# FFN gate and up products of blocks 2 to 6: seven block products in place of eight

## The reference

```python
def block(x, W_qkv, b_qkv, W_out, b_out):               # x: (2, 1024, 512) float32
    x = x + causal_attention(layernorm(x), 16 heads of 32) @ W_out.T + b_out
    h = layernorm(x)
    return x + (silu(h @ w_gate.T) * (h @ w_up.T)) @ w_down.T   # w_gate, w_up: (2048, 512)
```

## Time and profile before

| | before |
|---|---|
| median of 3 runs | 2179.28 us (2178.76 to 2180.1) |
| profiled execution, its own time | 2179.44 us |
| its span | 2177.7 us |
| TensorE matmul busy | 2113.8 us, 97% |
| VectorE busy | 1253.6 us, 58% |
| ScalarE busy | 530.9 us, 24% |
| GpSimd busy | 668.9 us, 31% |
| mean granted TensorE clock | 0.997 |

### The profile page before, as it was taken

The page is one execution under the profiler, slowest core; times in us unless marked ns, Lnnn a source line. Parts: engine busy times, 40 slices in busy tenths (PEclk is TensorE's granted clock), DMA queues, the critical chain, the costliest instruction groups (busy, mean ns, idle before and its releaser), DMA issues.

```text
span 2177.7 us, 34223 instructions
## 1 busy us (share of the span) xinstructions
PE 2113.8 (97%) x11056; PEld 1486.4 (68%) x11056; DVE 1253.6 (58%) x2476; ACT 530.9 (24%) x1076; POOL 668.9 (31%) x508
## 2 busy tenths in 40 slices
PE   6999999999999999999989999999999999999998
PEld 5555478888755548888865554888877554588886
DVE  6766564544676647444467665644456767454445
ACT  1344420000144441000014454100011444310001
POOL 3324233332312323323231233333323223233322
PEclk9999999999999999999999999999999999999999
DMA  4333111111323211111242321111113232111113
GB/s 130 94 79 79 31 36 52 49 58 39 79 70 79 70 31 49 50 48 49 68 129 70 79 69 40 39 59 39 49 40 81 68 81 68 40 49 49 59 39 97
DMA packets 59748, 135.15 MB, mean 62 GB/s; under 512 B 10784, under 2 KB 11808, under 8 KB 59552
## 3 DMA queue, kind: packets, MB, share of 16 engines
q1 hardware_dynamic: 59552, 132.71, 21.6%
HBM read 77.62 MB, written 4.19 MB: 38 GB/s over the span
## 4 chain that ended last, share of the span: by engine, by line
PE 88%; issue 5%; DVE 2%; POOL 2%; ACT 1%; DMA 1%; SPq 0%; DVEq 0%; POOLq 0%; ACTq 0%
PE ring L898 13%; PE ring L899 13%; PE ring L900 13%; PE bank L1011 13%; PE ring L965 8%; PE bank L989 7%; PE bank L898 7%; PE bank L900 7%; PE bank L899 7%; PE ring L889 1%; ACT prob L560 1%; DMA area<-nm_lo 1%; POOL area L438 1%; DVE xn L699 1%; POOL prob L463 1%
## 5 line engine op out<-in xcount | busy, mean ns | idle before, releaser
L898 PE MATMUL ring<-xt_hi,area 128*128 128x512 f32 x1248 | 489.8, 392 | 1.1 <-DVE kq_parts L688 1.1
L899 PE MATMUL ring<-xt_lo,area 128*128 128x512 f32 x1248 | 486.4, 390 | 0.0
L900 PE MATMUL ring<-xt_hi,area 128*128 128x512 f32 x1248 | 486.0, 389 | 0.0
L699 DVE CUSTOM_DVE_ANT_0 xn<-ring,mask_row 128x128 bf16<-128x128 f32 (+7 forms) x512 | 374.5, 749 | 99.9 <-PE ring L965 93.9
L560 ACT ACTIVATE prob<-bank 128x512 f32<-128x512 f32 (+3 forms) x768 | 335.0, 489 | 342.4 <-PE bank L989 341.6
L436 POOL TENSOR_SCALAR area<-w_stage 128x1024 fp32r<-128x1024 f32 x131 | 144.4, 1103 | 762.2 <-PE bank L900 404.7
L766 DVE TENSOR_TENSOR prob<-prob,ring 128x512 f32<-128x512 f32 x128 | 87.8, 686 | 456.9 <-ACT prob L578 456.9
L438 POOL TENSOR_TENSOR area<-w_stage,area 128x1024 fp32r<-128x1024 f32 x131 | 322.8, 2464 | 10.9
L578 ACT ACTIVATE prob<-ring 128x512 f32<-128x512 f32 x128 | 76.5, 598 | 970.4 <-PE ring L900 970.4
L898 PEld LDWEIGHTS ring<-xt_hi,area 128*128 128x128 f32 x1248 | 234.3, 188 | 59.1 <-issue 9.8
L900 PEld LDWEIGHTS ring<-xt_hi,area 128*128 128x128 f32 x1248 | 234.3, 188 | 49.1
(11 more groups left out here) (78 smaller groups left out, 2053.4 us busy)
## 6 DMA issues: line engine op xcount, KB each, us to landing
w_stage<-ffn_w SPq DMA_DIRECT2D x96, 512.0 KB, 3.3
area<-kq_parts SPq DMA_DIRECT2D x336, 128.0 KB, 2.4
w_stage<-attn_w SPq DMA_DIRECT2D x35, 512.0 KB, 3.3
x<-x_in SPq DMA_DIRECT2D x24, 256.0 KB, 3.9
area<-attn SPq DMA_DIRECT2D x48, 128.0 KB, 2.3
out<-x SPq DMA_DIRECT2D x16, 256.0 KB, 2.2
bias_rows<-row_bias SPq DMA_DIRECT2D x10, 256.0 KB, 4.2
area<-nm_hi SPq DMA_DIRECT2D x32, 8.0 KB, 1.8
```

The costliest lines, as they stand in the source:

```text
L699: dve.tensor_tensor_reduce(out=sum_out[:, RING[name] % 2, 0:keys], in0=src[:, 0:keys], in1=mask_row[:, TOKENS - keys:], scale=1.0, scalar= ...
L898: pe.matmul(dst, ah, bh, start=first and k == 0, stop=False)
L899: pe.matmul(dst, ah, bl, start=False, stop=False)
L900: ins = pe.matmul(dst, al, bh, start=False, stop=last and k == n - 1)
```

## The change

Let W be the weight of a block (gate or up), cut into W11, W12, W21, W22 (tile by half of the 512 inputs), and X the transposed x, cut into halves by chunks. For blocks 2 to 6 ("quads") both steps of a block are formed together by Winograd's form of the 2x2 product with seven products of 6 matmuls each:

- GpSimd forms S1 = W21 + W22, S3 = W11 - W21, S2 = S1 - W11, S4 = W12 - S2 from the staged weight (four 256-column instructions) and splits the four sums as it splits a weight (`quad_sums`, `s_split`), ahead of the plain split of the same slot. The sums lie in a ring of four buffers.
- VectorE forms four differences of X in six 1024-column instructions (`diff_sum`), ScalarE their high parts, VectorE their low parts (`diff_to_lo`, 1024 columns, four of them). They are put between the steps 2 and 3 (`DIFFS_BESIDE`). For their sake `xt_to_hi` writes a second, full copy of the late half of x^T (`xt_late`), ahead of the high part.
- TensorE sums m1, m6, m5, m3 up in one PSUM pair ("x"), m7 and m4 in a second ("y"), m2 alone in a third ("z"). ScalarE copies the state of x behind m1, m6 and m5 to SBUF (`keep`); VectorE adds these copies to y, z and y (`quad_add`). ScalarE makes the high part of the hidden tiles (`quad_hi`).
- The down rows of a block follow in the next block, behind m7, m6, m5 and m2, in two PSUM banks in place of four. Those of block 6 stand between and behind the gate_up of step 14.
- At the end of an iteration GpSimd writes ones over 2 x 6144 elements again, since the sums have lain there.

```diff
+PRODUCTS = ("m1", "m7", "m6", "m5", "m2", "m3", "m4")
+OUTPUTS = ((1, 1), (0, 0), (0, 1), (1, 0))
+DIFFS_BESIDE = ((((("sum", 0), ("sum", 1)), (("sum", 2), ("sum", 3), ("lo", 0))),
+                ((("sum", 4), ("lo", 1)), (("sum", 5), ("lo", 2)))))
+ROWS_BEHIND = ("m7", "m6", "m5", "m2")
...
 def xt_to_hi(it, name):
+                if name in (("ln2", 2), ("ln2", 3)):
+                    late = xt_late[:, :, 2 * (r - 2) * P:2 * (r - 1) * P].rearrange("p k (t n) -> p k t n", n=P)
+                    act.activation(late, src, ACT.Copy)
                 act.activation(dst, src, ACT.Copy).then_inc(xt_hi_ready, 1)
...
 def split_weights(it, i):
+                if part < 2 and QUAD_FIRST <= b <= QUAD_LAST:
+                    quad_sums(it, b, part, w_stage[:, j % 2, :])
+                    s_split(it, b, part)
...
+                pool.tensor_tensor(s1, a21, a22, ALU.add).then_inc(s_step, 1)
+                pool.tensor_tensor(s3, a11, a21, ALU.subtract).then_inc(s_step, 1)
+                wait_alone(pool, s_step, s_steps(it, b, w, 0))
+                pool.tensor_tensor(s2, s1, a11, ALU.subtract).then_inc(s_step, 1)
+                wait_alone(pool, s_step, s_steps(it, b, w, 2))
+                pool.tensor_tensor(s4, a12, s2, ALU.subtract).then_inc(s_step, 1)
...
+                pool.tensor_scalar(both[:, 0, :, :], sums, 1.0, 0.0, ALU.mult, ALU.add
+                                   ).then_inc(s_step, 1)
+                pool.tensor_tensor(both[:, 1, :, :], sums, both[:, 0, :, :].bitcast(F32),
+                                   ALU.subtract)
...
                 for i in range(FFN_SLOT0 + 3, SLOTS + 2):
                     split_weights(it, i)
+                wait_alone(pool, product_full, products(it, QUAD_LAST, "m3", 1))
+                wait_alone(pool, w_split, it * SLOTS + SLOTS + 2)
+                pool.memset(k_stack[3 * HEAD:3 * HEAD + 2, 1:, :, :].bitcast(F32), 1.0).then_inc(ones_ready, 1)
...
 # VectorE
+                def quad_block(b):
+                    add_rows(2 * b - 1)
+                    quad_add(b, (1, 1), 0)
+                    quad_add(b, (1, 1), 1)
+                    if b > QUAD_FIRST:
+                        add_rows(2 * b - 2, range(2))
+                    quad_multiply(b, (1, 1))
+                    quad_add(b, (0, 0), 0)
+                    quad_add(b, (0, 0), 1)
+                    quad_lo(b, (1, 1))
+                    if b > QUAD_FIRST:
+                        add_rows(2 * b - 2, range(2, CT))
+                    quad_multiply(b, (0, 0))
+                    quad_lo(b, (0, 0))
+                    quad_multiply(b, (0, 1))
+                    quad_lo(b, (0, 1))
+                    quad_add(b, (1, 0), 0)
+                    quad_add(b, (1, 0), 1)
+                    quad_multiply(b, (1, 0))
+                    quad_lo(b, (1, 0))
...
+                for s in range(1, QUAD_STEPS[0]):
                     for t in range(BT):
                         hidden_parts(s, t)
+                        if s >= QUAD_STEPS[0] - 2:
+                            for what, n in DIFFS_BESIDE[s - QUAD_STEPS[0] + 2][t]:
+                                (diff_sum if what == "sum" else diff_to_lo)(n)
                     for d in downs_after(s):
+                        add_rows(d)
+                diff_to_lo(3)
+                for block_at in range(QUAD_FIRST, QUAD_LAST + 1):
+                    quad_block(block_at)
...
 # TensorE
+                    if m == "m1":
+                        pe.wait_ge(w_split, it * SLOTS + FFN_SLOT0 + 3 * b + w + 1)
+                        if b == QUAD_FIRST:
+                            pe.wait_ge(rows_drained, rows_taken(it, row_at(2 * b - 2, w)))
...
+                    rows = [late[0:2], late[2:4], [(2 * b - 2, 0), (2 * b - 2, 1)], [(2 * b - 2, 2), (2 * b - 2, 3)]]
+                    if b == QUAD_FIRST:
+                        rows = [[one] for one in late]
+                    for m in PRODUCTS:
+                        for w in range(2):
+                            product(b, m, w)
+                        if m in ROWS_BEHIND:
+                            for s, t in rows[ROWS_BEHIND.index(m)]:
+                                down_row(s, t)
...
+                for b in range(QUAD_FIRST, QUAD_LAST + 1):
+                    quad_block(b)
+                for t in range(BT):
+                    gate_up(STEPS - 2, t)
+                    down(STEPS - 4 + t)
+                down(STEPS - 2)
```

More of the change, by code:

```diff
@@ L85, in downs_after @@
 def downs_after(s):
-    return {0: (0,), 1: (), STEPS - 2: (s - 1, s), STEPS - 1: (s,)}.get(s, (s - 1,))
+    return {0: (0,), 1: ()}.get(s, (s - 1,))
 EARLY = {1: 2, 3: 12, 5: 12, 7: 12}
@@ L137, in ring_order @@
     yield from (("gu", 0, 0), ("gu", 0, 1), ("ln2", 2), ("ln2", 3))
-    yield from (("gu", s, t) for s in range(1, STEPS) for t in range(BT))
+    yield from (("gu", s, t) for s in range(1, STEPS) for t in range(BT) if s not in QUAD_STEPS)
 TAKE_AFTER = (8, 17)
@@ L424, in split_weights @@
                     after = last_product(before)
-                    if after[0] == "rows":
+                    if after[0] == "product":
+                        wait_alone(pool, product_full, products(it, *after[1:]))
+                    elif after[0] == "rows":
                         wait_alone(pool, rows_full, it * ROWS + after[1] + 1)
@@ L449, in last_product @@
                 x_last = b * CHUNKS + CHUNKS - 1
-                return ("rows", x_last * CT + CT - 1) if part == 2 else ("gu", x_last, BT - 1)
+                if part == 2:
+                    return "rows", max(row_at(b * CHUNKS + c, CT - 1) for c in range(CHUNKS))
+                return ("product", b, "m4", part) if QUAD_FIRST <= b <= QUAD_LAST else ("gu", x_last, BT - 1)
             def inverse_deviation(it, ln, c):
@@ L755, in add_projected, with add_rows @@
                     tile_stats(t)
-                def add_rows(row, t, b):
-                    dve.wait_ge(rows_full, it * ROWS + row + 1)
-                    dve.tensor_tensor(x[:, t, :], x[:, t, :], bank[b][:, :], ALU.add).then_inc(rows_drained, 1)
+                def add_rows(s, tiles=range(CT)):
+                    for n in tiles:
+                        dve.wait_ge(rows_full, it * ROWS + row_at(s, n) + 1)
+                        t = s % CHUNKS * CT + n
+                        dve.tensor_tensor(x[:, t, :], x[:, t, :], row_bank(s, n)[:, :], ALU.add
+                                          ).then_inc(rows_drained, 1)
@@ L892, in iteration, with three @@
             def iteration(it):
-                def three(dst, terms, first=True, last=True):
+                def three(dst, terms, first=True, last=True, more=False):
                     n = len(terms)
                     for k, (ah, al, bh, bl) in enumerate(terms):
-                        pe.matmul(dst, ah, bh, start=first and k == 0, stop=False)
-                        pe.matmul(dst, ah, bl, start=False, stop=False)
-                        ins = pe.matmul(dst, al, bh, start=False, stop=last and k == n - 1)
+                        pe.matmul(dst, ah, bh, start=first and k == 0, stop=False, skip_group_check=more)
+                        pe.matmul(dst, ah, bl, start=False, stop=False, skip_group_check=more)
+                        ins = pe.matmul(dst, al, bh, start=False, stop=last and k == n - 1, skip_group_check=more)
                     return ins
@@ L1046, in gate_up @@
                     pe.wait_ge(ring_drained, buffer_free(it, ("gu", s, t)))
+                    if s == STEPS - 2:
+                        quads_left(1 + t)
                     for w in range(2):
@@ L1053, in down @@
                 def down(s, tiles=range(BT)):
[L1054 to L1057, removed]
                     for t in range(CT):
[L1059 to L1070, removed]
+                        down_row(s, t, tiles)
@@ L1161, in iteration @@
                     down(0, range(t, t + 1))
-                for s in range(1, STEPS - 1):
+                for s in range(1, QUAD_STEPS[0]):
                     for t in range(BT):
```

255 lines of the change are left out of this document (241 added, 14 removed).

## The result

The changed kernel takes 2212.76 us (median of 4, 2212.38 to 2219.56) against 2179.02 before: a ratio of 1.0163, 95% interval 1.0147 to 1.0179. It is slower by 34 us, where 2182 was forecast with a range that ended at 2210. The profiled execution took 2212.88 us, its span is 2210.8.

What follows compares the result with a forecast made beforehand. TensorE, busy 97% of the span, was taken as the bound. -54.4 + 35.2 (entry) + 6.4 (clock) + 3.2 (FFN start) + 12.0 (exit) = +2.4 on 2179.44 gave 2181.8, stated as 2182 us; 8-in-10 range 2138 to 2210.

Steps and rivals of the forecast that it cites:

- What is removed: Gate and up of five blocks: 240 matmul slots fewer, 54.4 us saved; a quad lasts 29.92 us.
- GpSimd in a quad: Quads: 256-column two-input instruction 0.73 us, 28.2 of 29.92 us filled per block, no stall from GpSimd in quads 3 to 6.
- Rival 2: Quads: GpSimd becomes the bound, m1 waiting for weights; 2202 us at 1.0 us per sum, 2219 at 1.1; chance 0.19.
- Entry: Before the first m1: GpSimd's 22.6 and VectorE's 13.7 us add up from 324.3; wait 8.8 us per iteration, 35.2 in all.
- Exit: Behind quad 6: a down row waits for the last hidden tile's low part, 3.0 us late, 12.0 in all.
- Start of the FFN: ScalarE's extra 1024-column copy ahead of the high part delays TensorE by 0.8 us, 3.2 in all.
- VectorE and ScalarE in a quad: Inside the quads: VectorE about 15 us, ScalarE 8.4 us; smallest margin 1.6 us in the hidden tiles' chain, no stall.
- The clock term: Behind the entry wait: about eight matmuls at the lower clock, 1.6 us each time, 6.4 in all, bounds 0 and 12.8.

Runs made afterwards that it cites:

- e1: Changed kernel with GpSimd's weight sums and their split left out, TensorE taking plain weight parts instead; 2198.8 us (ratio 1.0099 to the kernel before).
- e7: Changed kernel with VectorE's additions of down(2)'s rows taken ahead of the last difference sum and its low part; 2206.5 us (ratio 1.0120).
- e4: Changed kernel with the six difference sums moved to step 1, their high parts with them, and low parts spread behind hidden tiles; 2177.7 us (ratio 0.9995).
- e3: Changed kernel with both gate_up tiles of step 14 placed before down(12) behind the last quad; 2195.8 us (ratio 1.0077).
- e2: Changed kernel with the first quad's down rows in pairs behind m7 and m6, not one behind each of four products; 2195.6 us (ratio 1.0081).
- e5: Changed kernel with 36 matmuls without use put into the wait in front of the first m1; 2205.0 us (ratio 1.0118).
- e8: Changed kernel with GpSimd's sums and their split replaced by constant writes that read nothing, TensorE taking plain weight parts; 2194.2 us (ratio 1.0068).
- e6: Changed kernel with the edits of e2, e3 and e4 together; 2135.3 us (ratio 0.9800).

## Why the prediction was wrong, point by point

- *What is removed*: right; 240 matmuls, 29.92 us per quad.
- *GpSimd in a quad*: right. A 256-column instruction takes 0.73 to 0.75 undisturbed (0.73 forecast), and a block keeps GpSimd busy for 24.5 us in quads that TensorE never waits in (28.2 forecast, gaps and waits included). Rival 2 is refuted as the cause, though the time lies where it would have put it: the list has no wait for a weight part.
- *Entry*: the wait is 8.6 us per iteration (8.8 forecast), 34.2 in all (35.2). The size was right, the reason only in part, and so the close hit is in part luck. The sum added up the work of two engines from 324.3 on. It left out that the last tile's chain can't start before its gate and up products are done. Without GpSimd's sums and their split it would have given no wait at all (324.3 + 9.6 + 13.7 + 0.6 = 348.2, ahead of 353.1), and e1 still measured 5.1. So the sums' backlog is 3.5 of the 8.6, and the rest is an order without slack that meets plain splits: e7 takes 3.3 away by order alone, e4 7.5 by order and place together. (The sum also has five casts where its own count of 18 instructions leaves four, 0.28 too much.)
- *Exit*: 3.2 us per iteration, 12.7 in all (12.0); e3 confirms the place.
- *Start of the FFN*: 2.0 in all (3.2).
- *VectorE and ScalarE in a quad: "The smallest margin is 1.6 us: no stall"*: this step failed. It was worked out for a quad whose rows come in pairs, and carried over to the first quad, whose four rows are spread to behind m2 while VectorE's order keeps them all in front of `quad_add`. I had the edit in the diff (`rows = [[one] for one in late]`) and followed only its weight place, not the queue behind it. Cost: four waits of 3.15 (12.6 us), 1.0 for m6 once, and 10.1 us of slowed matmuls behind them, some 24 of the 31 us that the forecast is off by. e2 shows it.
- *The clock term*: mis-sized. I took 6.4 us, for the entry alone, with 12.8 as its upper end; measured are 25.4 in the four stages. By place they are 8.6 at the entry, 10.1 at the second quad and 6.3 at the exit. At the entry the price was near (1.6 each forecast, 1.9 by e5, 2.0 to 2.4 by the trace), but it is paid after short waits too: behind the exit's 3.2 us in all four iterations, behind the second quad's 3.15 us in three of four. The sentence that the shorter exit wait may not pay, which I drew from the Trainium skill (TensorE: Matmul & The Clock Gate, "What's actually happening"), does not hold here: 3.2 us were enough.

The sum, mended with these: -54.4 + 62.5 + 25.4 = +33.5 where +2.4 stood. Of the missing 31, 14 are the second quad's waits and 19 the clock; entry and exit differ by 1, and against these stand the 3.2 of the FFN's start, which the +2.4 has and the 62.5 has not. What remains open is why a wait of one length sometimes leaves the clock alone. It isn't bound to the place: the second quad's wait left it alone in the first iteration of the changed kernel, but halved it there in e1, e3, e4, e5 and e7, and the exit's left it alone in two iterations of e4 and one of e1. That e2 saved 17 us where its FFN stages fell by 22 is the part outside the stages, which is 5.2 us longer in its trace. Whether the changed kernel's own low 1173.5 there is chance or an effect of the change, no run shows.

## What to carry to other kernels

Where a change takes matmuls off a TensorE that never pauses, look first at the seams, in front of the first and behind the last of the new pieces, and ask which of its waits have no slack there. In this kernel the steady state was covered from the first version on. Follow each queue there by itself, with its own order; a piece that differs from the others by one line has a chain of its own. Put VectorE's work with two SBUF inputs where GpSimd doesn't read SBUF, and price waits of TensorE like those met here (2.9 to 8.7 us) at their length plus 1.3 to 3.3 us for the clock, which nearly all of them cost.

## What the runs showed of the hardware that I had not expected

- GpSimd's memset of 1440 columns (about 1.4 us each) leaves VectorE's two-input subtractions at 1.22 us, but a cast from SBUF to SBUF waits for it (1.33 us in place of 0.43, and 3.83 with the split before it).
- Waits of TensorE of 3.2 us were enough to halve its clock in 7 of 8 cases of the changed kernel. Over the traces of e1 to e5, e7, e8 and the changed kernel, waits of 2.9 to 3.3 us in front of the quads, in the second quad and behind the last did it in 53 of 58 cases; e4's four and e6's four of 1.2 us never did.
- A wait of 5.2 us cost as many half-rate matmuls as one of 8.6 (41 against 40 behind the four entries). Filling the wait with matmuls without use gave 7.8 us back.
